# Picks' two-part rows laid out by contraction slice, picked ends compared on GpSimd, and the first four weight units split in another order

## The chip, the cores and the metric

The kernel runs on one core of one Trainium2 chip. The metric is the device time of one execution in microseconds (us), taken as the median of several runs. A profile is one further execution whose instructions are recorded; its own span and time stand beside the median below. The engines are TensorE (PE, with its weight loads as PEld), VectorE (DVE), ScalarE (ACT), GpSimd (POOL) and the queue engine SyncE (SP).

## The reference, cut to what matters

A graph network layer on 256 nodes with 8192 edges is followed by a feed-forward layer with 256 routed experts. Only the first 1024 edges have edge weights of their own kind: 128 "hh", 640 "oo", 256 "ho".

```python
x = x + gnn(layernorm(x)); x = x + ffn(layernorm(x))
# gnn, n_f = layernorm(x), 256 x 1024
feat = concatenate([n_f[edge_src], n_f[edge_dst]], axis=1)          # per edge, 2048 wide
e_hh = relu(feat[:128] @ W_hh + b_hh)                               # W_hh is 2048 x 1024
e_oo = relu(feat[128:768] @ W_oo + b_oo)
e_ho = relu(feat[768:] @ W_ho + b_ho)                               # here: all the rest
logit = (e_f @ W_a + b_a)[:, 0]; alpha = softmax of logit over edges with the same dst
z_f = segment_sum(alpha * n_f[edge_src], edge_dst)
new = relu(concatenate([n_f, z_f]) @ W_hn + b_hn)  (first 64 nodes),  W_on, b_on (the others)
# ffn: top-4 experts of 256 by hashed keys, each silu(x @ down) @ up
```

The change touches the first tile of 128 edges, which alone uses W_hh, and what stands beside it.

## The kernel before, in words

Every float32 product is made of two parts: a value is split into a high part (rounded to the type fp32r) and a low part (value minus high part), and three products (high x high, low x high, high x low) are summed in PSUM.

**Weights** come in 20 units of 4096 columns on 128 partitions. Unit u goes to slot s = u % 2 as its n-th use, n = u // 2. SP loads it in two halves into `raw`; ACT makes each half's high part (`hi(s, n)`, line 583, into `whi`), DVE the low part (`lo(s, n)`, line 795, into `wlo`), and TensorE may then use it. SP's wait before loading the next use of a slot half is for DVE's `lo` of the half before (lines 436 and 437). Units 0 to 3, which are `(0,0)`, `(1,0)`, `(0,1)`, `(1,1)` as slot and use, hold W_hh; the two W_hh halves for source and destination are uses 0 and 1.

**The first tile's features.** DVE makes the layer norm `nf` (line 826). TensorE turns `nf` by 8 transposes per tile of 128 nodes (`turn(0, t)`, line 1257), for all later edges. For the first 128 edges, a one-hot matrix `head_pick` (in the buffer `ohx`) of the 128 source and 128 destination numbers is made by four compares (`pick`, line 842, DVE), and `nf` split in `nf_hi` (ACT, line 589) and `nf_lo` (DVE, line 850), both in slot 1 of `wlo`. 32 matmuls of 256 columns (line 1278) give the features, already turned: for each of 8 contraction slices c, two node tiles t and two parts. The stationary operand is a slice with a step of 8 numbers (32 bytes) through a row of `nf_hi` or `nf_lo`. After slices 0 to 3 and again after 4 to 7 ACT takes the high part of the features to `tab_dst` (line 593) and DVE the low part (line 856).

**The first tile's edges.** TensorE multiplies the features with units 0 and 1 (48 matmuls of 512 columns, lines 1287 to 1289), turns the edge numbers, multiplies with units 2 and 3 (48 more), adds the bias, and then starts `project(1, 0)` with unit 4. DVE then runs `dot(0)` (line 988), sorts the other edges into buckets (`in_windows`, up to line 882), and TensorE counts them (line 1333) after two slices of `project(1, 0)` and ranks them (lines 1340 to 1346) after four; ACT and DVE go on from the ranks (lines 623, 900 to 918).

**Order.** Each engine's order is written out by hand; there is no scheduler. `turn_hi`/`turn_lo` (lines 574, 833) are the two parts of the turned `nf`. GpSimd starts with two long broadcasts of edge numbers by its own DMA queue (line 475, 320 KB each, into `idx_b`), makes the constants, and later compares (line 518) and runs its own long loops (lines 532 to 544).

## Time and profile before

| what | value |
|---|---|
| median of 3 runs | 761.04 us (759.07 to 761.8) |
| time of the profiled execution | 758.95 us |
| its span | 757.2 us |
| PE busy | 710.9 us, 94% of the span |
| DVE, ACT, POOL busy | 510.9, 367.0, 215.3 us |
| shares of the chain that ended last (page, part 4) | PE 64%, POOL 14%, DVE 8%, ACT 6% |
| bytes read from HBM | 112.74 MB |

A time in the rows below is in us from the start of the span. The profiled execution is 2.1 us under the median of the runs, and 1.75 us lie between its span and its time. Line numbers are those of the kernel printed above.

### The profile page before, as it was taken

How to read it: one execution, taken by the hardware profiler on the slowest of the kernel's cores; microseconds unless marked ns; L12 is line 12 of the kernel's file. 1: busy time of each engine (PE TensorE's matmuls, PEld its weight loads, DVE VectorE, ACT ScalarE, POOL GpSimd, SP SyncE). 2: the span in 40 equal slices, each digit the busy share in tenths (PEclk: the TensorE clock that was granted, in tenths of full speed). 3: DMA queues.
4: the chain of work that ended last, by engine and by line, in shares of the span. 5: the costliest groups of instructions: out<-in, count | busy, mean ns of one | idle time of the engine just before them, and what ended most of it. 6: DMA issues, size and time to landing. Idle time of an engine off the chain costs nothing.

```text
span 757.2 us, 9554 instructions
## 1 busy us (share of the span) xinstructions
PE 710.9 (94%) x3325; PEld 560.4 (74%) x3325; DVE 510.9 (67%) x706; ACT 367.0 (48%) x435; POOL 215.3 (28%) x329
## 2 busy tenths in 40 slices
PE   3999999997979989899799999999999999999998
PEld 3877776785555656587677888888888888888886
DVE  6897797597999999638878464544564544565543
ACT  3754989647646653017435244343344343344340
POOL 3373668798898804800000000000000000000000
PEclk9999999999989999699979999999999999999999
DMA  8785233341000006406905645456645356645411
GB/s 317 277 319 216 112 111 113 112 177 46 1 1 1 0 1 235 167 0 239 316 14 178 238 142 191 148 201 222 212 137 192 144 201 222 220 137 188 157 73 57
DMA packets 50058, 114.21 MB, mean 151 GB/s; under 512 B 2245, under 2 KB 35397, under 8 KB 44906
## 3 DMA queue, kind: packets, MB, share of 16 engines
q1 hardware_dynamic: 49418, 112.95, 41.5%
q0 software_dynamic: 160, 0.66, 0.2%
q8 instruction: 18, 0.29, 0.2%
q10 hardware_dynamic: 448, 0.20, 0.1%
q14 instruction: 14, 0.11, 0.0%
HBM read 112.74 MB, written 1.05 MB: 150 GB/s over the span
## 4 chain that ended last, share of the span: by engine, by line
PE 64%; POOL 14%; DVE 8%; issue 6%; ACT 6%; DMA 2%; DVEq 0%; SPq 0%; ACTq 0%
PE ps L1287 18%; PE ps L1289 17%; PE ps L1288 17%; POOL peak L539 5%; POOL oh_src L541 4%; POOL pen L544 4%; PE ps L1257 3%; DVE wlo L795 3%; ACT chunk_col L641 2%; PE ps L1587 1%; ACT chunk_gap L636 1%; PE ps L1523 1%; ACT whi L583 1%; DMA raw<-n_L_ffn_values_down_dram 1%; PE ps L1278 1%
## 5 line engine op out<-in xcount | busy, mean ns | idle before, releaser
L795 DVE TENSOR_TENSOR wlo<-raw,whi 128x2048 fp32r<-128x2048 f32 x104 | 235.3, 2288 | 67.1 <-ACT whi L583 66.3
L583 ACT ACTIVATE whi<-raw 128x2048 fp32r<-128x2048 f32 x104 | 195.9, 1911 | 90.7 <-PE ps L1289 65.9
L1287 PE MATMUL ps<-whi,nT 128*128 128x512 f32 x392 | 156.2, 399 | 1.4 <-ACT act_g L758 1.4
L1289 PE MATMUL ps<-wlo,nT 128*128 128x512 f32 x392 | 152.9, 390 | 0.0
L1288 PE MATMUL ps<-whi,nT 128*128 128x512 f32 x392 | 152.8, 390 | 0.0
L988 DVE SCALAR_TENSOR_TENSOR ps<-ps,xt 128x1024 f32<-128x1024 f32 x80 | 97.5, 1219 | 5.9 <-PE ps L1313 5.0
L1287 PE MATMUL ps<-whi,gT_hi 128*128 128x512 f32 x240 | 93.6, 390 | 0.0
L1289 PE MATMUL ps<-wlo,gT_hi 128*128 128x512 f32 x240 | 93.4, 389 | 0.0
L1288 PE MATMUL ps<-whi,gT_lo 128*128 128x512 f32 x240 | 93.4, 389 | 0.0
L1221 DVE TENSOR_TENSOR gw<-act_g,route 128x512 f32<-128x512 f32 x32 | 20.7, 688 | 106.8 <-ACT act_g L758 106.8
L1287 PEld LDWEIGHTS ps<-whi,nT 128*128 128x128 f32 x392 | 73.6, 188 | 18.3 <-issue 2.3
L1289 PEld LDWEIGHTS ps<-wlo,nT 128*128 128x128 f32 x392 | 73.6, 188 | 15.8
L1288 PEld LDWEIGHTS ps<-whi,nT 128*128 128x128 f32 x392 | 73.7, 188 | 14.3
L758 ACT ACTIVATE act_g<-ps 128x1024 f32<-128x1024 f32 x16 | 16.4, 1028 | 126.3 <-PE ps L1289 126.3
L1311 PE MATMUL ps<-tab_src,ring 128*128 x148 | 66.7, 450 | 11.2 <-DVE ps L988 5.2
L532 POOL TENSOR_SCALAR chunk_col<-iota,keep 128x74 f16<-128x74 f16 x58 | 52.5, 926 | 32.3 <-DVE keep L918 16.5
L1313 PE MATMUL ps<-tab_dst,ring 128*128 x148 | 60.1, 406 | 0.0
L1287 PEld LDWEIGHTS ps<-whi,gT_hi 128*128 128x128 f32 x240 | 45.0, 188 | 9.6 <-issue 0.4
L1289 PEld LDWEIGHTS ps<-wlo,gT_hi 128*128 128x128 f32 x240 | 45.0, 188 | 9.4
L1288 PEld LDWEIGHTS ps<-whi,gT_lo 128*128 128x128 f32 x240 | 45.0, 188 | 9.3
L1311 PEld LDWEIGHTS ps<-tab_src,ring 128*128 128x128 f32 x148 | 29.1, 197 | 30.6 <-issue 26.0
L539 POOL TENSOR_SCALAR peak<-iota,slot_idx 128x64 f16<-128x64 f16 x74 | 39.4, 532 | 11.1 <-DVE slot_idx L957 4.5
(268 smaller groups left out, 928.1 us busy)
## 6 DMA issues: line engine op xcount, KB each, us to landing
raw<-n_L_ffn_values_down_dram SPq DMA_DIRECT2D x16, 2048.0 KB, 8.3
raw<-in_L_ffn_values_up_dram SPq DMA_DIRECT2D x16, 2048.0 KB, 7.5
raw<-in_L_gnn_W_hh_dram SPq DMA_DIRECT2D x8, 1024.0 KB, 8.9
raw<-in_L_gnn_W_oo_dram SPq DMA_DIRECT2D x8, 1024.0 KB, 6.0
raw<-in_L_gnn_W_ho_dram SPq DMA_DIRECT2D x8, 1024.0 KB, 4.7
raw<-in_L_gnn_W_hn_dram SPq DMA_DIRECT2D x8, 1024.0 KB, 4.8
raw<-in_L_gnn_W_on_dram SPq DMA_DIRECT2D x8, 1024.0 KB, 5.1
xt<-in_x_dram SPq DMA_DIRECT2D x4, 512.0 KB, 7.3
```

Source lines behind the costliest of these rows:

```text
L532: last = nc.gpsimd.tensor_scalar(chunk_col[:, n % 2, j % CHUNK, 0:WN], iota16[:, 0:WN], keep[:, 2, j:j + 1], keep[:, 0, j:j + 1], ALU.is_e ...
L539: nc.gpsimd.tensor_scalar(same[:, w % 2, :], iota16[:, 1:NH + 1], slot_idx[:, 1, w:w + 1], None, ALU.is_equal).then_inc(win_same, 1)
L541: nc.gpsimd.tensor_scalar(oh_src[:, w, :], iota16[:, 1:NH + 1], slot_idx[:, 0, w:w + 1], None, ALU.is_equal).then_inc(win_src, 1)
L544: nc.gpsimd.tensor_scalar(pen[:, w, :], same[:, w % 2, :], 1.0, -NEVER, ALU.subtract, ALU.mult).then_inc(win_pen, 1)
L583: nc.scalar.activation(half(whi, s, j, down), half(raw, s, j, down), ACT.Copy)\
L795: nc.vector.tensor_tensor(half(wlo, s, j, down), half(raw, s, j, down), half(whi, s, j, down).bitcast(F32), ALU.subtract)\
L988: nc.vector.scalar_tensor_tensor(out=bank(q, 2), in0=bank(q, 2), scalar=0.0, in1=wa_b[:], op0=ALU.max, op1=ALU.mult, accum_out=logit[:, i: ...
L1287: nc.tensor.matmul(o, a_hi, b_hi, start=start, stop=False)
L1288: nc.tensor.matmul(o, a_lo, b_hi, start=False, stop=False)
L1289: return nc.tensor.matmul(o, a_hi, b_lo, start=False, stop=stop)
L1311: nc.tensor.matmul(bank(q + h), hot[:, 0, :], src_rows[:, bass.ds(a + h * HALF, HALF)], start=True, stop=False)
L1313: last = nc.tensor.matmul(bank(q + h), hot[:, 1, :], dst_rows[:, bass.ds(b + h * HALF, HALF)], start=False, stop=True)
```

## The change

Four things are changed; line numbers of the new file differ by 9 to 15.

1. `nf_hi` and `nf_lo` are written in the order (slice c, row q): ACT and DVE read `nf` with a step of 8 numbers, and the stationary operand of the 32 picking matmuls is contiguous.
2. The four compares of `pick` go from DVE to GpSimd, at the end of its constants, and GpSimd's two long broadcasts are issued behind them.
3. TensorE does `turn(0, 1)` behind the picking matmuls instead of ahead of them.
4. ACT and DVE take the features' first half between the two halves of unit 0, and split unit 2 (ACT) and units 2 and 3 (DVE) before the parts of the turned `nf` and the bias.

```diff
-        nf_hi, nf_lo = (wlo[:, 1, NT * D * k:NT * D * (k + 1)].rearrange("p (t n) -> p t n", t=NT) for k in range(2))
+        nf_hi, nf_lo = (wlo[:, 1, NT * D * k:NT * D * (k + 1)].rearrange("p (t c q) -> p t c q", t=NT, c=C)
+                        for k in range(2))
+        nf_by_c = nf[:].rearrange("p t (q c) -> p t c q", c=C)
 # GpSimd
-            for a, ends in enumerate((src, dst)):
-                pool.dma_start(idx_b[:, a, P:HEAD * P], ends[P:HEAD * P].partition_broadcast(P))\
-                    .then_inc(batch_loaded, 16)
 ...  the constants
+            pool.wait_ge(first_batch, 32)
+            for a in range(2):
+                for j, number in enumerate((row_no[:, 0:1], node[:, 1:2])):
+                    last = nc.gpsimd.tensor_scalar(head_pick[:, j * N + a * P:j * N + (a + 1) * P], idx_b[:, a, 0:P],
+                                                   number, None, ALU.is_equal)
+            last.then_inc(picker_ready, 1)
+            for a, ends in enumerate((src, dst)):
+                pool.dma_start(idx_b[:, a, P:HEAD * P], ends[P:HEAD * P].partition_broadcast(P))\
+                    .then_inc(batch_loaded, 16)
 # ACT
-                nc.scalar.activation(nf_hi[:, t, :], nf[:, t, :], ACT.Copy).then_inc(nfhi_ready, 1)
-            hi(0, 0, first=True)
-            for h in range(2):
+                nc.scalar.activation(nf_hi[:, t, :, :], nf_by_c[:, t, :, :], ACT.Copy).then_inc(nfhi_ready, 1)
+            hi(0, 0, first=True, parts=(0,))
+            feature_hi(0)
+            hi(0, 0, first=True, parts=(1,))
+            feature_hi(1)
             hi(1, 0, first=True)
+            hi(0, 1)
             for t in range(NT):
                 turn_hi(0, t)
             act.wait_ge(small_loaded, 16 * 6)
             nc.scalar.activation(bias_hi[:], bias[:], ACT.Copy).then_inc(bias_ready, 1)
-            hi(0, 1)
             hi(1, 1)
 # DVE
-            pick()
-                nc.vector.tensor_tensor(nf_lo[:, t, :], nf[:, t, :], nf_hi[:, t, :].bitcast(F32), ALU.subtract)\
+                nc.vector.tensor_tensor(nf_lo[:, t, :, :], nf_by_c[:, t, :, :], nf_hi[:, t, :, :].bitcast(F32), ALU.subtract)\
-            lo(0, 0)
-            for h in range(2):
+            lo(0, 0, parts=(0,))
+            feature_lo(0)
+            lo(0, 0, parts=(1,))
+            feature_lo(1)
             lo(1, 0)
-            for t in range(NT):
-                turn_lo(0, t)
 ...
             lo(0, 1)
+            lo(1, 1)
+            for t in range(NT):
+                turn_lo(0, t)
             (bias_lo)
-            lo(1, 1)
 # TensorE
-            for t in range(NT):
-                turn(0, t)
+            turn(0, 0)
 ...
-                                                parts[part][:, t, :].rearrange("p (q c) -> p c q", c=C)[:, c, :],
+                                                parts[part][:, t, c, :],
 ...
+            turn(0, 1)
```

On TensorE, from its first transpose to the first matmul with W_hh. Before:

```order
L1257 MATMUL ps<-ident,nf 128x128 [waits norm_ready,consts]
L1257 MATMUL ps<-ident,nf 128x128 x7
L1257 MATMUL ps<-ident,nf 128x128 [waits norm_ready]
L1257 MATMUL ps<-ident,nf 128x128 x7
L1278 MATMUL ps<-ohx,wlo 128x256 [waits nflo_ready,picker_ready]
L1278 MATMUL ps<-ohx,wlo 128x256
L1278 MATMUL ps<-ohx,wlo 128x256 [waits nflo_ready]
L1278 MATMUL ps<-ohx,wlo 128x256 x29
L1287 MATMUL ps<-whi,tab_dst 128x512 [waits lo_ready0,featlo_ready,consts]
```

After:

```order
L1267 MATMUL ps<-ident,nf 128x128 [waits norm_ready,consts]
L1267 MATMUL ps<-ident,nf 128x128 x7
L1287 MATMUL ps<-ohx,wlo 128x256 [waits nflo_ready,picker_ready]
L1287 MATMUL ps<-ohx,wlo 128x256
L1287 MATMUL ps<-ohx,wlo 128x256 [waits nflo_ready]
L1287 MATMUL ps<-ohx,wlo 128x256 x29
L1267 MATMUL ps<-ident,nf 128x128 [waits norm_ready]
L1267 MATMUL ps<-ident,nf 128x128 x7
L1297 MATMUL ps<-whi,tab_dst 128x512 [waits lo_ready0,featlo_ready,consts]
```

The second group of eight transposes has moved behind the 32 picking matmuls.

On DVE, from the picks to the copy of the edge numbers ahead of unit 4 (`idx_col`). Before:

```order
L842 TENSOR_SCALAR ohx<-idx_b,small 128x128 [waits first_batch,consts]
L842 TENSOR_SCALAR ohx<-idx_b,small 128x128 x3
L850 TENSOR_TENSOR wlo<-nf,wlo 128x1024 [waits nfhi_ready] x2
L795 TENSOR_TENSOR wlo<-raw,whi 128x2048 [waits hi_ready0] x2
L856 TENSOR_TENSOR tab_dst<-ps,tab_dst 128x1024 [waits feathi_ready] x2
L795 TENSOR_TENSOR wlo<-raw,whi 128x2048 [waits hi_ready1] x2
L833 TENSOR_TENSOR nT<-ps,nT 128x8x128 [waits turned_hi] x2
L966 CAST idx_rowf<-idx_rows 64x256 [waits idx_loaded,consts]
L795 TENSOR_TENSOR wlo<-raw,whi 128x2048 [waits hi_ready0] x2
L969 TENSOR_TENSOR bias_lo<-bias,bias_hi 5x1024 [waits bias_ready]
L795 TENSOR_TENSOR wlo<-raw,whi 128x2048 [waits hi_ready1] x2
L972 COPY idx_col<-ps 128x128 [waits smallT]
```

After:

```order
L854 TENSOR_TENSOR wlo<-nf,wlo 128x1024 [waits nfhi_ready] x2
L810 TENSOR_TENSOR wlo<-raw,whi 128x2048 [waits hi_ready0]
L861 TENSOR_TENSOR tab_dst<-ps,tab_dst 128x1024 [waits feathi_ready]
L810 TENSOR_TENSOR wlo<-raw,whi 128x2048 [waits hi_ready0]
L861 TENSOR_TENSOR tab_dst<-ps,tab_dst 128x1024 [waits feathi_ready]
L810 TENSOR_TENSOR wlo<-raw,whi 128x2048 [waits hi_ready1] x2
L974 CAST idx_rowf<-idx_rows 64x256 [waits idx_loaded,consts]
L810 TENSOR_TENSOR wlo<-raw,whi 128x2048 [waits hi_ready0] x2
L810 TENSOR_TENSOR wlo<-raw,whi 128x2048 [waits hi_ready1] x2
L848 TENSOR_TENSOR nT<-ps,nT 128x8x128 [waits turned_hi] x2
L980 TENSOR_TENSOR bias_lo<-bias,bias_hi 5x1024 [waits bias_ready]
L982 COPY idx_col<-ps 128x128 [waits smallT]
```

The picks are gone, the features' first half stands between the halves of unit 0, and the turned `nf` and the bias stand behind unit 3. ACT's order moves in the same way, with the turned `nf` and the bias between units 2 and 3.

## Rows read from the trace of the kernel before

**Rows 1.** The chain that ended last: start, duration, what, with its count.

```profile
1.26 6.81 DMA xt<-in_x_dram
...
15.39 7.90 PE ps L1278 x32
...
53.42 0.56 PE ps L1333 x16
...
79.27 1.24 DVE tab_src L982
...
390.54 1.84 PE ps L1699 x16
```

**Rows 2.** Timeline of the start: start, duration, engine, line, operation, count, [idle before].

```profile
11.15 1.53 DVE L826 TENSOR_SCALAR nf<-xt,mv,ln 128x1024 f32<-128x1024 f32 x2
12.00 2.00 ACT L589 ACTIVATE wlo<-nf 128x1024 fp32r<-128x1024 f32 x2 [1.87 <-DVE nf L826]
...
12.60 0.87 DVE L842 TENSOR_SCALAR ohx<-idx_b,small 128x128 fp32r<-128x128 int32 x4
...
13.38 2.35 DVE L850 TENSOR_TENSOR wlo<-nf,wlo 128x1024 fp32r<-128x1024 f32 x2
...
23.32 1.03 ACT L593 ACTIVATE tab_dst<-ps 128x1024 fp32r<-128x1024 f32 x1 [2.81 <-PE ps L1278]
...
24.24 3.71 ACT L583 ACTIVATE whi<-raw 128x2048 fp32r<-128x2048 f32 x2
24.38 1.23 DVE L856 TENSOR_TENSOR tab_dst<-ps,tab_dst 128x1024 fp32r<-128x1024 f32 x1 [2.62 <-ACT tab_dst L593]
...
26.18 4.50 DVE L795 TENSOR_TENSOR wlo<-raw,whi 128x2048 fp32r<-128x2048 f32 x2 [0.57 <-ACT whi L583]
...
35.38 0.50 PE L1287 MATMUL ps<-whi,tab_dst 128*128 128x512 f32 x1 [0.78 <-DVE wlo L795]
```

**Rows 3.** Waits of DVE in the first 48 us: us in total, times, longest.

```profile
DVE tab_dst L856 <- ACT tab_dst L593: 2.8, 2, 2.6
...
DVE wlo L795 <- ACT whi L583: 0.8, 2, 0.6
```

**Rows 4.** By line and window: ns min/median/max, first and last start.

```profile
L1278 PEld LDWEIGHTS ps<-ohx,wlo x32: 312/337/341, 15.1 to 22.7; 128*128 128x128 f32 x32
...
L1257 PE MATMUL ps<-ident,nf x11: 273/417/417, 13.2 to 15.1; 128*128 128x128 f32 x11
...
L1257 PE MATMUL ps<-ident,nf x8: 421/421/478, 378.1 to 379.7; 128*128 128x128 f32 x8
...
L1257 PE MATMUL ps<-ident,nf x8: 270/274/276, 387.6 to 388.4; 128*128 128x128 f32 x8
...
L518 POOL TENSOR_SCALAR ohx<-idx_b,small x8: 602/1258/10582, 33.0 to 51.2; 128x128 fp32r<-128x128 int32 x8
```

**Rows 5.** DVE groups by shape: count | busy us, mean ns | idle before.

```profile
L914 DVE TENSOR_REDUCE slot<-place 128x58 f32<-128x928 f32 x1 | 1.9, 1862 | 0.0
...
L1111 DVE TENSOR_REDUCE peak<-oh_dst 128x74 f32<-128x592 f32 x1 | 0.8, 769 | 0.0
```

**Rows 6.** DMA: us to landing; GpSimd's queue in 6.5 to 8.1 (packets, MB, share).

```profile
idx_b<-in_dst_dram ACTq DMA_DIRECT2D x1, 64.0 KB, 7.1
...
q0 software_dynamic: 31, 0.16, 23.8%
...
raw<-in_L_gnn_W_hh_dram SPq DMA_DIRECT2D x1, 1024.0 KB, 4.7
...
raw<-in_L_gnn_W_oo_dram SPq DMA_DIRECT2D x1, 1024.0 KB, 6.1
```

**Rows 7.** Timeline of DVE behind the first tile's edges.

```profile
47.90 1.23 DVE L988 SCALAR_TENSOR_TENSOR ps<-ps,xt 128x1024 f32<-128x1024 f32 x1
...
51.13 1.12 DVE L882 TENSOR_TENSOR in_bucket<-bucket,iota 128x928 f16<-128x928 f32 x1
...
57.57 1.12 DVE L893 TENSOR_TENSOR earlier<-count,below 58x928 f16<-58x928 f16 x1
```

More of the change, by code:

```diff
@@ L588, in _, with feature_hi @@
                 act.wait_ge(norm_ready, t + 1)
-                nc.scalar.activation(nf_hi[:, t, :], nf[:, t, :], ACT.Copy).then_inc(nfhi_ready, 1)
-            hi(0, 0, first=True)
-            for h in range(2):
+                nc.scalar.activation(nf_hi[:, t, :, :], nf_by_c[:, t, :, :], ACT.Copy).then_inc(nfhi_ready, 1)
+            def feature_hi(h):
                 act.wait_ge(feat_done, h + 1)
@@ L834, in turn_lo, with feature_lo @@
                                         ALU.subtract).then_inc(turned_lo, 1)
-            def pick():
-                dve.wait_ge(consts, 6)
-                dve.wait_ge(first_batch, 32)
-                for a in range(2):
-                    for j, number in enumerate((row_no[:, 0:1], node[:, 1:2])):
-                        last = nc.vector.tensor_scalar(head_pick[:, j * N + a * P:j * N + (a + 1) * P], idx_b[:, a, 0:P],
-                                                       number, None, ALU.is_equal)
-                last.then_inc(picker_ready, 1)
             layer_norm(1, range(NT))
-            pick()
             for t in range(NT):
                 dve.wait_ge(nfhi_ready, t + 1)
-                nc.vector.tensor_tensor(nf_lo[:, t, :], nf[:, t, :], nf_hi[:, t, :].bitcast(F32), ALU.subtract)\
+                nc.vector.tensor_tensor(nf_lo[:, t, :, :], nf_by_c[:, t, :, :], nf_hi[:, t, :, :].bitcast(F32), ALU.subtract)\
                     .then_inc(nflo_ready, 1)
-            lo(0, 0)
-            for h in range(2):
+            def feature_lo(h):
                 dve.wait_ge(feathi_ready, h + 1)
```

## The prediction

> **What bounds the kernel now.** I read the chain that ended last first. Of its shares on the page (in the table above) TensorE holds 64% and GpSimd 14%, nearly all of it behind the stage that is changed. In its pieces by time [rows 1], in the first 24 us the chain runs over the second half of x (landed at 8.07), the layer norm and the picking matmuls: 7.90 us for 32, or 247 ns each, of only 256 columns. The reader should see that this is far from TensorE's price for 256 columns: 1.84 us for 16 later ones, 115 ns each [rows 1]. The by-line view tells why: the weight load of a picking matmul takes 337 ns, and its stationary operand is read with a step of 32 bytes [rows 4].
>
> Then comes the timeline of the start [rows 2] and DVE's waits [rows 3]. In the first 48 us DVE waits only for ACT in its own chain behind the layer norm, 2.8 + 0.8 = 3.6 us; all else from the second `nf_lo` (ends 15.73) to `dot(0)` (47.90) [rows 2, 7] is work, 32.2 - 3.6 = 28.6 us. TensorE waits 0.78 us, for DVE, ahead of unit 2 [rows 2]. So both must be followed: a stage given to TensorE is worth something only if DVE's `dot(0)` also comes earlier.
>
> The place where both meet is the bucket count. DVE has `in_bucket` ready at 51.13 + 1.12 = 52.25, TensorE begins to count at 53.4, a slack of 1.1 us; the ranking waits for 57.57 + 1.12 = 58.69 and TensorE comes at 59.6, slack 0.9 [rows 1, 7]. What follows hangs on the ranks: ACT, DVE's sort, then the four `tab_src` parts, the last ending at 80.5 [rows 1], for which TensorE waits. So **the shift of the ranking is the shift of the end**, unless the later GpSimd loop changes it.
>
> **The change part by part.**
>
> *The long broadcasts.* GpSimd's queue moved 0.16 MB between 6.5 and 8.1 us, 24% of the DMA engines' time [rows 6]; x's second half landed at 8.07. Without it x lands earlier: 24% of 1.6 us, 0.4 us. Bounds are 0 and 1.3 (8.09 less 6.80, where DVE has done the first half of x). I take 0.4. The broadcasts are now issued near 11 us and first needed beyond 40 us (ACT's unit 3, GpSimd's `head_destinations`); a queue time of 11 us would still cover that. Behind them on GpSimd stands only `both_ready`.
>
> *The compares.* DVE loses 0.87 us [rows 2], but `nf_lo` waits for ACT's `nf_hi`, so 0.3 us at most is won. GpSimd's unobstructed price is 0.60 us [rows 4]: from the landing at 1.27 + 7.1 = 8.4 [rows 6] four take until 10.8. They are needed at 15. Cost nothing, covered by `nf_lo`. If the cover goes, see the third rival.
>
> *The strided reads* go from TensorE to ACT and DVE. No row shows either engine reading single words 32 bytes apart. The nearest is a reduction over a step of 232 bytes: 1.862 us for 928 numbers, 2.0 ns each, against 0.769 for 592 in order, 1.3 each [rows 5], so 0.7 ns more for each. Bounds for `nf_lo`: 1.22 (today) and 2.6 (today's doubled, and a little); I take 1.22 + 1024 x 0.7 ns = 1.9. For `nf_hi`: 1.05 to 2.1; with no row of ACT I take a third of the way, 1.4. The Trainium skill speaks against the change here: "SBUF — State Buffer" (its remark on cachelines) says that each access that crosses to a new 16-byte line pays, and "Vector Engine (DVE) Microarchitecture Reference", 5.2, gives 1.73 ns per column with one source hopping every element. By that `nf_lo` would take 1.85 us and the sum would stand; a reader who trusted the old 1.22 would forecast 1.8 us less for it.
>
> With x 0.4 earlier ACT starts at 11.6: `nf_hi` ends at 13.0 and 14.4, `nf_lo` at 14.95 and **16.8** (before 15.73).
>
> *The picking matmuls.* Two run at 15, the other 30 from 16.85. What is their price? Before, TensorE worked without a pause from 12.1, and its transposes fell from 417 to 273 ns shortly before 15 us [rows 4]. 421 ns is the same transpose at granted clock 0.50 and 274 at 1.00, at 378 and 388 us; so it rose from 1.2 to 2.4 GHz there, and all picking ran at 2.4. After, TensorE has eight transposes, then almost nothing until 16.85. I take it that it is at 1.2 GHz until about 20: 256 columns in 0.213 us. Bounds: 0.115 at once, and 0.215 to the end. Then feature half 0 is done at 16.85 + 14 x 0.213 + 0.15 = 20.0 (before 19.4), half 1 at 21.9, and the eight transposes at 22.7. So contiguous rows gain 0.7 on the whole, not 4.2.
>
> *The features between the halves.* ACT takes half 0 by 21.05 (1.03 each); DVE, done with unit 0's first half at 19.05, idles 2.05 us; its part ends at 22.35. TensorE starts W_hh at 22.8 (23.1 before). ACT splits the second half of unit 0 by 22.95, so DVE idles 0.65 more. Unit 0 ends on DVE at 25.3, feature half 1 at 26.5, unit 1 at 30.95 (before 26.18 + 4.50 = 30.7).
>
> *The other order.* DVE is done with unit 2 at 35.7. The second half of unit 2 is issued only when unit 0 is done, at 25.3 (before about 20.4), and lands after 4.7 to 6.1 us [rows 6]; I take 5.0. ACT then does it by 32.2, the turned `nf` (two of 1.0, as half a feature takes) and the bias by 35.1, unit 3's first half by 37.0: DVE idles 1.3 us. Idle in all: 2.05 + 0.65 + 1.3 = 4.0, and `dot(0)` comes at 16.8 + 28.6 + 4.0 = 49.4, allowing 0.2 for the hand-overs 49.6, **1.7 later**. TensorE loses its 0.78 wait and starts `project(1, 0)` at 47.5 (47.7 before); it then waits for DVE's buckets, 49.6 + 4.35 = 54.0, beyond its 53.2. What is late next is DVE, and 1.1 and 0.9 us of its delay fall into the slack named above: 1.7 - 0.9 = **+0.8 at the ranking**, +0.1 for the restart of TensorE behind the wait. GpSimd's eight compares, 19.9 us before, begin near 43 instead of 33 and end near 63, ahead of the sort's 69.
>
> **The sum** against the profiled execution: 758.95 + 0.9 = 759.85. That execution lies 2.1 us below the median of the runs, so I forecast 761.9.
>
> **The rivals.**
>
> *1. The strided reads cost nothing.* For it: ACT and DVE have no strided row at 32 bytes; against it the reduction's row and TensorE's own 337 ns. `nf_lo` ends at 15.1, all moves 1.7 earlier, features at half clock still: `dot(0)` 47.6, ranking 1.0 before today's. If TensorE is at 2.4 GHz too, half 0 is done 1.3 us sooner, and with x 1 us earlier the ranking is 3 us before. Time 760.0, to 758.0 at the best.
>
> *2. Strided reads at twice the price, loads at 6.1 us.* `nf_hi` 2.1, `nf_lo` 2.6: it ends near 20, half 0 at 22.3, `dot(0)` at 52 to 53: +3 to +4.2. It decides from the point where `nf_lo` ends beyond 16, since DVE has no other slack before `dot(0)` than 0.9. 764.0 to 765.3.
>
> *3. The compares come late (slower).* GpSimd's compares range from 602 to 10582 ns, the longest while DVE ran its `lo` back to back [rows 4]: DVE shuts it out. They start at 8.4 and must be through before `nf_lo` starts at 13; the margin is 2.2 us, with DVE's `nf` (11.15 to 12.7) in it [rows 2]. If one compare is left then, it lies until DVE's first pause, near 19.5, and the picking begins there: 2.7 us later than in my sum, features 3.3 later, time 765.2. "SBUF — State Buffer", on who interferes with whom, in the Trainium skill, states such a lock for two SBUF inputs; the 10.58 us agree.
>
> *4. It doesn't do what it says:* TensorE's pace at 1.2 GHz makes contiguous loads worthless, nothing else changes: picking 32 x 0.215, half 0 as in the sum, half 1 at 23.4. DVE decides anyway; 762.2, inside the forecast.
>
> **How the numbers follow.** Forecast with its neighbour 4: 0.55, 760.5 to 763.2. Rival 1: 0.22. Rival 2: 0.10. Rival 3: 0.06. Something that I see no row for, half to each side: 0.07. GpSimd's loop from 142 to 264, whose locked-out compares fall differently, and the runs' own spread of 2.7 us add about a microsecond either way. The range 758.5 to 764.6 leaves out rival 3, most of 2 and the best of 1. 0.5% is 3.8 us, about what can be told from no change: faster (below 757.2) 0.11, slower (above 764.8) 0.11, same 0.78.
>
> **What would show it.** Right: `nf_hi` near 1.4 and `nf_lo` near 1.9; picking matmuls at two paces, 0.21 then about 0.12; DVE idle for ACT in three places, one ahead of unit 3; a TensorE wait for `in_bucket`; `dot(0)` near 49.6. Wrong: a changed duration nowhere but in the weight loads (rival 1), a compare of several us (rival 3), or an end that moves by another amount than the ranking. The forecast fails most easily at the two prices taken between far bounds, ACT's strided read and the clock.

## The result and the profile after

| | before | after |
|---|---|---|
| median of 20 runs each, on one chip | 760.12 us (758.06 to 762.33) | 763.04 us (760.62 to 767.68) |
| ratio, with its 95% interval | | 1.0041 (1.0028 to 1.0053) |
| time and span of the profiled execution | 758.95, 757.2 us | 760.62, 758.9 us |
| PE busy | 710.9 us | 707.1 us |

The change makes the kernel slower by 0.4%, 2.9 us between the medians: within the 0.5% called "same", but its interval lies wholly above 1. The forecast was +0.9 us, 761.9 us with a range of 758.5 to 764.6. Range and sign held; the size is three times what the sum gave. That the time itself is only 1.1 us above the forecast is in part luck: the forecast started from a median before of 761.04 us, and the 20 runs of the comparison gave 760.12.

The chain that ended last of the kernel after (start, duration, what) answers to [rows 1]:

```profile
1.25 7.42 DMA xt<-in_x_dram
...
12.68 2.14 ACT wlo L598
14.84 4.00 DVE wlo L854 x2
18.89 3.33 PE ps L1287 x14
...
30.64 2.29 DVE wlo L810
32.95 6.43 DMA raw<-in_L_gnn_W_hh_dram
39.40 1.93 ACT whi L592
```

Before, TensorE's 32 picks stood in this chain with 7.90 us. Now ACT's and DVE's parts of `nf` stand there, then only the first 14 picks behind them, and later a weight load, `raw`, directly ahead of ACT's and DVE's split of it. x itself landed 0.6 us later than before (7.42 us where 6.81 stood).

The timeline of the kernel after, for the same pieces as [rows 2] and [rows 7] (start, duration, engine, line, names, [idle before]):

```profile
11.84 1.54 DVE L841 TENSOR_SCALAR nf<-xt,mv,ln 128x1024 f32<-128x1024 f32 x2
12.68 4.08 ACT L598 ACTIVATE wlo<-nf 128x1024 fp32r<-128x1024 f32 x2 [1.87 <-DVE nf L841]
14.84 3.99 DVE L854 TENSOR_TENSOR wlo<-nf,wlo 128x1024 fp32r<-128x1024 f32 x2 [1.47 <-ACT wlo L598]
...
23.30 1.22 DVE L861 TENSOR_TENSOR tab_dst<-ps,tab_dst 128x1024 fp32r<-128x1024 f32 x1 [2.26 <-ACT tab_dst L603]
25.09 2.29 DVE L810 TENSOR_TENSOR wlo<-raw,whi 128x2048 fp32r<-128x2048 f32 x1 [0.57 <-ACT whi L592]
38.67 2.29 DVE L810 TENSOR_TENSOR wlo<-raw,whi 128x2048 fp32r<-128x2048 f32 x1 [1.15 <-ACT whi L592]
41.36 2.29 DVE L810 TENSOR_TENSOR wlo<-raw,whi 128x2048 fp32r<-128x2048 f32 x1 [0.39 <-ACT whi L592]
51.57 1.21 DVE L998 SCALAR_TENSOR_TENSOR ps<-ps,xt 128x1024 f32<-128x1024 f32 x1
54.67 1.12 DVE L890 TENSOR_TENSOR in_bucket<-bucket,iota 128x928 f16<-128x928 f32 x1
61.18 1.12 DVE L901 TENSOR_TENSOR earlier<-count,below 58x928 f16<-58x928 f16 x1
```

Read it against the old rows in order. `nf` is 0.69 us later (11.15 before). Each `nf_hi` takes 2.04 us where 1.0 stood, each `nf_lo` 2.0 where 1.2 stood, so the second `nf_lo` ends at 18.8 instead of 15.73: 3.1 us late. `dot(0)` is 3.67 us later, `earlier`, which the ranking needs, 3.61.

TensorE's weight loads of the picking matmuls show why contiguous rows gave it little at first. The line view of the kernel after (ns min/median/max, first and last start), from 12 to 22 us and from 22 to 24 us:

```profile
L1287 PEld LDWEIGHTS ps<-ohx,wlo x17: 285/330/338, 17.0 to 21.8; 128*128 128x128 f32 x17
...
L1287 PEld LDWEIGHTS ps<-ohx,wlo x16: 188/192/287, 21.8 to 23.7; 128*128 128x128 f32 x16
```

The contiguous load takes 330 ns until about 22 us, hardly less than the 337 ns of the strided one in [rows 4], and 192 ns after that. The profile prints a granted clock of 1.00 for the whole stretch, so the clock is read from durations here. By the pair of transposes in [rows 4], 421 and 274 ns at granted clock 0.50 and 1.00, TensorE is at 1.2 GHz first and at 2.4 GHz from about 22 us: its eight transposes ahead of the picks take 421 ns, those behind them 276. It did those first eight, sat idle for 2.25 us, did two picks and sat idle for 1.13 more. The 330 ns need not be the price of the load alone: the weight loads of the transposes are recorded with 0.22 to 0.23 us in the same slow stretch, and no run separates a load from the matmul that it overlaps.

The ranking gives each edge its place in its bucket; DVE's first operation with these ranks is `total_i`. It starts 2.78 us later than before, and what follows on DVE up to the GpSimd loop between 2.7 and 2.8. The profiled execution gave 1.1 us of this back behind 180 us; its granted clock from 290 to 400 us was 0.91 where the one before had 0.89. The medians, 2.9 us apart, don't show such a gift.

### The profile page after: what moved, and what is told of

It reads as the page before. It is cut to its first block, busy times and chain, and to the rows that moved or that the text cites. A ratio compares the mean times of both kernels' runs of the same rounds, so it can differ in the third digit from the quotient of the medians.

```text
span 758.9 us, 9553 instructions
## 1 busy us (share of the span) xinstructions
PE 707.1 (93%) x3325; PEld 556.5 (73%) x3325; DVE 511.9 (67%) x702; ACT 369.0 (49%) x435; POOL 212.6 (28%) x333
## 3 DMA queue, kind: packets, MB, share of 16 engines
HBM read 112.74 MB, written 1.05 MB: 150 GB/s over the span
## 4 chain that ended last, share of the span: by engine, by line
PE 59%; POOL 14%; DVE 10%; ACT 6%; issue 6%; DMA 4%; DVEq 0%; SPq 0%; ACTq 0%
PE ps L1297 17%; PE ps L1299 16%; PE ps L1298 16%; POOL peak L548 5%; POOL pen L553 5%; POOL oh_src L550 4%; DVE wlo L810 4%; PE ps L1267 2%; ACT whi L592 2%; ACT chunk_col L656 2%; ACT chunk_gap L651 1%; PE ps L1597 1%; DMA raw<-n_L_ffn_values_down_dram 1%; PE ps L1632 1%; DMA xt<-in_x_dram 1%
## 5 line engine op out<-in xcount | busy, mean ns | idle before, releaser
L1299 PEld LDWEIGHTS ps<-wlo,nT 128*128 128x128 f32 x392 | 73.6, 188 | 15.8
L541 POOL TENSOR_SCALAR chunk_col<-iota,keep 128x74 f16<-128x74 f16 x58 | 52.5, 922 | 26.5 <-PE ps L1366 15.8
```

The costliest lines, as they stand in the source:

```text
L541: last = nc.gpsimd.tensor_scalar(chunk_col[:, n % 2, j % CHUNK, 0:WN], iota16[:, 0:WN], keep[:, 2, j:j + 1], keep[:, 0, j:j + 1], ALU.is_e ...
L1299: return nc.tensor.matmul(o, a_hi, b_lo, start=False, stop=stop)
```

## The experiments

Twelve experiments ran, in three groups of four; two of them repeat a kernel. The column "ranks, shift" gives the start of `total_i` against 62.11 us in the kernel before; it and the two columns to its left are read from one profile each.

| kernel | second `nf_lo` ends | `dot(0)` | ranks, shift | ratio to before (95%) |
|---|---|---|---|---|
| before | 15.7 | 47.90 | 0 | 1 |
| after | 18.8 | 51.57 | +2.78 | 1.0041 (1.0028 to 1.0053) |
| after_again | 19.0 | 52.96 | +4.17 | 1.0033 (1.0019 to 1.0046) |
| after_old_rows | 16.2 | 49.63 | +0.84 | 1.0015 (1.0000 to 1.0029) |
| before_rows_only | 18.1 | 49.22 | +1.32 | 1.0002 (0.9982 to 1.0021) |
| after_old_order | 18.8 | 49.50 | +1.61 | 1.0023 (1.0011 to 1.0035) |
| before_order_only | 15.8 | 49.29 | +0.51 | 1.0008 (0.9994 to 1.0023) |
| after_early_broadcast | 18.1 | 50.89 | +2.11 | 1.0018 (1.0006 to 1.0030) |
| before_picks_only | 16.1 | 48.67 | +0.77 | 1.0003 (0.9989 to 1.0017) |
| before_unit2_first | 15.6 | 47.84 | -0.05 | 0.9997 (0.9984 to 1.0011) |
| high_parts_first | 15.7 | 46.51 | -1.38 | 0.9987 (0.9970 to 1.0004) |
| high_first_again | 15.7 | 46.50 | -1.39 | 0.9964 (0.9952 to 0.9977) |
| high_first_by_slice | 18.5 | 48.34 | +0.44 | 1.0001 (0.9986 to 1.0015) |
| high_first_bias_pool | 15.7 | 47.27 | -1.38 | 0.9986 (0.9973 to 0.9999) |

A ratio has an interval of about 1 us either way. The shift of the ranks comes from one profile: in the two of high_parts_first it agrees to 0.01 us, in the two of the kernel after it differs by 1.4 us, for a reason found below (the landing of one load). Shift and ratio agree within the ratio's interval but for after_again, whose profile is slower than its ratio, and high_first_again, whose ratio is better than its shift.

### Part by part: the rows and the order

My theory after the result (A) was that the strided reads on ACT and DVE are the loss, and only because the new order leaves nothing to cover them; the rival (B) was that the order alone is. I undid each in the kernel after and did each alone in the kernel before.

**after_old_rows**, part 1 undone:

```diff
-nc.scalar.activation(nf_hi[:, t, :, :], nf_by_c[:, t, :, :], ACT.Copy)
+nc.scalar.activation(nf_hi[:, t, :], nf[:, t, :], ACT.Copy)
 ...  nf_lo and the stationary operand in the same way
```

> The kernel after, with part 1 undone: nf_hi and nf_lo written in nf's own order, the picking matmuls' weight loads with a step of 32 bytes. The whole computation stays. Theory A (the price of the strided reads on ACT and DVE, 2.09 and 2.02 us where 1.0 and 1.2 stood, is the loss, because in the new order nothing covers it): the second nf_lo ends near 16.4 instead of 18.8, the features' first low part starts near 21 instead of 23.3, dot(0) near 49 to 50 instead of 51.6, the ranking 0 to 1.3 us behind that of the kernel before; median 0 to 1.3 us above before (ratio 1.000 to 1.002). Theory B (the new order of units alone is the loss, DVE waits for ACT in it whatever the rows cost): dot(0) stays within 0.7 us of 51.6, median 2.5 to 3 us above before (1.0035 to 1.004). Open beside it: the pace of strided picking matmuls at a granted clock of half speed, 0.24 us apart if the loads are hidden there, 0.35 or more if not.

`nf_lo` ends at 16.2 and the ranks come 1.94 us earlier than in the kernel after. Theory A's numbers hold (49.63, +0.84), and theory B, which had `dot(0)` within 0.7 us of 51.6, is wrong. The open question has an answer too, in the chain and line views:

```profile
L1285 PEld LDWEIGHTS ps<-ohx,wlo x32: 312/338/341, 15.2 to 23.2; 128*128 128x128 f32 x32
```

```profile
16.23 7.53 PE L1285 MATMUL ps<-ohx,wlo 128*128 128x256 f32 x30 [0.22 <-DVE wlo L852]
```

Thirty strided picks take 7.53 us, 0.25 each. Of the contiguous ones in the kernel after the first 14 took 3.33 us, 0.24 each, and the other 16 the 1.9 us that were left of 5.23, 0.12 each. So in the slow stretch contiguous rows are worth next to nothing to TensorE, and behind it half of a pick. How long the slow stretch lasts is not the layout's doing: 30 contiguous picks took 5.23 us in the kernel after, but 6.51 in after_early_broadcast below, where they began 0.7 us earlier and loads of 330 ns lasted until about 24 us.

**before_rows_only**, part 1 alone:

```diff
-nc.scalar.activation(nf_hi[:, t, :], nf[:, t, :], ACT.Copy)
+nc.scalar.activation(nf_hi[:, t, :, :], nf_by_c[:, t, :, :], ACT.Copy)
 ...  nf_lo and the stationary operand in the same way
```

> The kernel before with part 1 alone (rows by contraction slice). The whole computation stays. Theory A in its full form (the price matters only together with the new order): nf_lo ends near 18.2 instead of 15.7, 2.5 us later, but DVE's 2.6 us wait ahead of the features' first low part shrinks to near 0, since it splits all of unit 0 meanwhile; unit 1 ends on DVE near 31.0 (30.7 before), dot(0) near 48.2 to 48.5, the ranking at most 0.1 us later; median within 0.5 us of before (ratio 0.9995 to 1.0007). A rival, A2 (the price comes through in any order): dot(0) at 50 or later, median 1.5 to 2.5 us above before (1.002 to 1.0033). Theory B: no change, as A.

The expectation misreads a row: DVE's wait of 2.6 us in the kernel before stands ahead of the second low part of the features, at 24.38 in [rows 2], and ahead of the first there is one of only 0.2:

```profile
20.54 1.23 DVE L856 TENSOR_TENSOR tab_dst<-ps,tab_dst 128x1024 fp32r<-128x1024 f32 x1 [0.21 <-ACT tab_dst L593]
```

In before_rows_only the long one shrank to 1.80 us, and not to nothing, since the second half of the features came 1.3 us later:

```profile
18.21 6.38 PE L1280 MATMUL ps<-ohx,wlo 128*128 128x256 f32 x30 [1.12 <-DVE wlo L852]
```

```profile
22.66 1.23 DVE L858 TENSOR_TENSOR tab_dst<-ps,tab_dst 128x1024 fp32r<-128x1024 f32 x1
24.62 1.03 ACT L595 ACTIVATE tab_dst<-ps 128x1024 fp32r<-128x1024 f32 x1 [2.00 <-PE ps L1280]
25.68 1.22 DVE L858 TENSOR_TENSOR tab_dst<-ps,tab_dst 128x1024 fp32r<-128x1024 f32 x1 [1.80 <-ACT tab_dst L595]
```

The picks began 2.8 us later than in [rows 1] and saved only 1.5 of it; the ranks are 1.32 us late, `dot(0)` 49.22. So A's "only together with the order" is wrong, and A2's "50 or later" as well. The ratio, 1.0002, can't show 1.3 us but doesn't exclude it either (its upper end is 1.6 us).

**after_old_order**, part 4 undone, and **before_order_only**, part 4 alone (the diff shows the undoing):

```diff
-            hi(0, 0, first=True, parts=(0,))
-            feature_hi(0)
-            hi(0, 0, first=True, parts=(1,))
-            feature_hi(1)
+            hi(0, 0, first=True)
+            (both halves of the features)
 ...  the turned nf and the bias back ahead of unit 2, on DVE in the same way
```

> The kernel after with part 4 undone on ACT and DVE (both halves of unit 0 ahead of the features, the turned nf and the bias where they stood), and parts 1 to 3 kept. The whole computation stays. Theory A: nf_lo still ends near 18.8, but DVE's unit 0 covers the wait for the features: unit 1 ends near 31.5 (30.7 before, 32.9 after), dot(0) near 48.8, the ranking 0 to 0.2 us later than before; median 0 to 0.5 us above before. Rival A2 (the price comes through in any order): dot(0) near 50.5 or later, median 2 us or more above before. Theory B: median as before.

> The kernel before with part 4 alone on ACT and DVE. The whole computation stays. nf_lo ends at 15.7 as before. Theory A (order and price together): DVE has an idle stretch of about 2.5 us behind the first half of unit 0 as it has one of 2.6 now, unit 1 ends near 30.9, and no wait of over 0.5 us ahead of unit 3; dot(0) near 48.2, median within 0.5 us of before. Theory B (the order alone is the loss): DVE waits for ACT in three places, dot(0) at 50 or later, median 2 to 3 us above before.

Undone, the ranks come 1.17 us earlier; alone, 0.51 us later. Neither theory's numbers hold. Undone, A had `dot(0)` near 48.8 and the ranks at most 0.2 us late, A2 had 50.5 or later, and B a median as before; measured were 49.50, +1.61 and a ratio of 1.0023. Alone, A had 48.2 and B 50 or later, and 49.29 was measured. A had put the order alone at nothing and B the rows alone; both have a price of their own. The timeline of before_order_only shows the order's:

```profile
36.21 2.29 DVE L800 TENSOR_TENSOR wlo<-raw,whi 128x2048 fp32r<-128x2048 f32 x1 [0.87 <-ACT whi L583]
39.08 2.29 DVE L800 TENSOR_TENSOR wlo<-raw,whi 128x2048 fp32r<-128x2048 f32 x1 [0.57 <-ACT whi L583]
```

DVE waits for ACT ahead of both halves of unit 3, and `dot(0)` is 1.39 us late; 0.9 of it goes into the slack ahead of the ranking.

### The landing of x

In five profiles with the long broadcasts behind GpSimd's constants, x's second half reached DVE at 8.65 to 8.84 us; in those with the broadcasts in front, at 7.89 to 8.21 (nine profiles by the end). I had forecast the opposite.

**after_early_broadcast**:

```diff
 # GpSimd, ahead of the constants
+            for a, ends in enumerate((src, dst)):
+                pool.dma_start(idx_b[:, a, P:HEAD * P], ...).then_inc(batch_loaded, 16)
 ...  the constants, the four compares
-            for a, ends in enumerate((src, dst)):
-                pool.dma_start(idx_b[:, a, P:HEAD * P], ...).then_inc(batch_loaded, 16)
```

> The kernel after with GpSimd's two long broadcasts in front again, its four compares still behind the constants; the whole computation stays. In the three kernels with the late broadcasts DVE began on x's second half at 8.65 to 8.72, in the three with early ones at 8.04 to 8.10. Theory X (the early broadcasts do not delay x, their absence does): x's second half at 8.05 to 8.1, nf 0.6 us earlier than after, compares still through by 12.5, dot(0) near 51.0, the ranking 2.2 us behind that of before instead of 2.8, median 1.5 to 2.6 us above before. Rival X2 (what shifts x is GpSimd's own compares or its constants, not the queue): x at 8.65 or later, median as after, about 2.9 us above. Rival X3 (my first forecast: a broadcast ahead costs x 0.4 us): x at 9.0.

**before_picks_only**, part 2 alone:

```diff
-            layer_norm(1, range(NT))
-            pick()
+            layer_norm(1, range(NT))
 ...  the compares on GpSimd behind its constants, the broadcasts behind them
```

> The kernel before with part 2 alone (the four compares on GpSimd at the end of its constants, the long broadcasts behind them); the whole computation stays. Theory X: x at 8.65 to 8.7, nf 0.6 us later, nf_lo without the 0.3 us of the picks: ends near 16.0; features, unit 1 and the ranking 0.3 to 0.6 us later; median 0.3 to 0.6 us above before (ratio 1.0004 to 1.0008). Rival (the compares block or are blocked for longer): a compare of over 1 us, or nf_lo at 17 or later.

The chain's row on x, in after_early_broadcast and then in before_picks_only:

```profile
1.26 6.61 DMA xt<-in_x_dram
```

```profile
1.26 7.42 DMA xt<-in_x_dram
```

Moving nothing but the two broadcasts to the front brings x 0.8 us earlier and the ranks from +2.78 to +2.11; in the kernel before, compares and late broadcasts together cost 0.77 (0.3 to 0.6 expected), with x's row at 7.42 again. Theory X holds, X2 and X3 fall, and so does my first term (0.4 us the other way). In the window from 5.5 to 8.0 us the kernels before and after compare so (us, busy time and count of PE, PEld, DVE, ACT and POOL, granted clock, DMA share, GB/s):

```profile
5.50:8.00 2.50, 0.00 (x0) 0.00 (x0) 1.29 (x2) 0.00 (x0) 1.82 (x11) 1.00 0.73 241
```

```profile
5.50:8.00 2.50, 0.00 (x0) 0.00 (x0) 1.29 (x2) 0.00 (x0) 1.50 (x9) 1.00 0.68 195
```

There is 0.11 MB less traffic in all, but the early broadcasts themselves moved 0.14 MB in that window. What SP's own queue had moved when x's second half landed says more (packets, MB, share), in the kernel before up to 8.07 us and in the kernel after up to 8.67:

```profile
q1 hardware_dynamic: 305, 1.19, 46.8%
```

```profile
q1 hardware_dynamic: 341, 1.48, 51.7%
```

x is 1.05 MB of each (two loads of 512 KB). So before it landed, 0.14 MB of what SP had queued behind it, mostly weights, had been moved in the kernel before, and 0.43 MB in the kernel after. after_early_broadcast, the kernel after with the broadcasts in front, stood at 1.16 MB when x landed at 7.87 us. At 8.07 us, where x was complete in the kernel before, SP's queue had moved no less in the kernel after, 1.27 MB. So with the broadcasts behind, x does lose its share, to what SP itself has queued behind it. Why the early broadcasts hold that back, no run here tells; that stays open.

### Who sets the ranking, and a better version

**before_unit2_first** took one piece of part 4:

```diff
-            for t in range(NT):
-                turn_hi(0, t)
-            (bias_hi)
             hi(0, 1)
+            for t in range(NT):
+                turn_hi(0, t)
+            (bias_hi)
             hi(1, 1)
 ...  on DVE in the same way
```

> The kernel before with one piece of part 4: ACT and DVE split unit 2 ahead of the two parts of the turned nf and the bias, but leave these ahead of unit 3. The whole computation stays. In the kernel with all of part 4 DVE waited 0.87 us ahead of unit 3, because ACT still had the turned nf and the bias to do. Theory C (TensorE sets the ranking in the kernel before, DVE has 0.9 us in hand, and it is unit 3 ahead of the turned nf that costs DVE its wait): TensorE's 0.78 us wait ahead of unit 2 is gone, DVE has no new wait over 0.3 us ahead of unit 3, project(1, 0) and the ranking 0.6 to 0.8 us earlier; median 0.5 to 0.9 us below before (0.9988 to 0.9993). Rival (any such move only trades one wait for another): DVE waits 0.8 us or more ahead of unit 3 all the same, median within 0.3 us of before or above it.

Theory C fell, and the wait of DVE that its rival named did not come either. TensorE's wait of 0.78 us ahead of unit 2 went, and one of 0.62 us for unit 3 took its place (chain, then timeline, of before_unit2_first):

```profile
35.20 2.27 DVE nT L833 x2
37.46 1.12 DVE bias_lo L969
38.59 2.21 DVE wlo L795
```

```profile
40.84 0.50 PE L1287 MATMUL ps<-whi,tab_dst 128*128 128x512 f32 x1 [0.62 <-DVE wlo L795]
```

DVE does the same work in another order and TensorE meets it one unit later. I conclude that the start gets shorter only if DVE's own chain does.

**high_parts_first** tries that. Its picks don't wait for `nf_lo`: each half takes the high parts of both tiles first. Four more things differ from the kernel before, all named in the last lines of the diff.

```diff
-            for c in range(C):
-                for t in range(NT):
-                    (wait for nf_lo of tile t) for part in range(2): matmul
+            for h in range(2):
+                for part, there in enumerate((nfhi_ready, nflo_ready)):
+                    for t in range(NT):
+                        (wait for there) for c in range(4 * h, 4 * h + 4): matmul
 ...  rows as before; compares on GpSimd, broadcasts in front; turn(0, 1) behind;
 ...  features between the halves of unit 0; unit 2 ahead of the turned nf
```

> A version meant to beat both, built on the kernel before. The whole computation stays. The rows keep nf's order (cheap reads on ACT and DVE); the compares are on GpSimd, broadcasts in front; TensorE takes in each half of the features first the high parts of both node tiles, then the low ones, so that its strided weight loads begin with nf_hi (13.0) and not with nf_lo; the second eight transposes behind; features between the halves of unit 0; unit 2 ahead of the turned nf, unit 3 behind it. Theory: what the start needs is picking that does not wait for nf_lo; picking from 13.8 at 0.25 us each, half 0 done at 17.8 (19.3 before), half 1 at 21.8 (23.3), DVE idle under 1.5 us ahead of the features, dot(0) near 46, TensorE the bound: W_hh from 22.8 without a wait, ranking 1.0 to 1.3 us earlier than before; median 758.6 to 758.9 beside 759.9. Rival (the restart at half speed and the compares on GpSimd give it back): half 0 at 19 or later, median as before.

```profile
13.92 7.97 PE L1283 MATMUL ps<-ohx,wlo 128*128 128x256 f32 x32
```

```profile
19.13 1.23 DVE L857 TENSOR_TENSOR tab_dst<-ps,tab_dst 128x1024 fp32r<-128x1024 f32 x1 [0.79 <-ACT tab_dst L600]
```

The picks take the same 8 us but start at 13.92 instead of 15.1 [rows 4]. DVE's waits for ACT behind the layer norm come to 0.40 + 0.39 + 0.79 + 0.58 + 0.42 = 2.6 us, where [rows 3] had 3.6, and its compares are gone. The ranks come 1.38 us earlier, 0.1 us more than the upper end of the forecast. Of this, 0.55 us is the start of TensorE on W_hh, 22.56 instead of 23.11, and 0.78 us the wait ahead of unit 2, which is gone. The picks by parts were not tried without the other four moves, so their own share isn't shown.

**high_first_again** is the same kernel once more, beside **after_again**, the kernel after (no edit in either):

> The kernel of high_parts_first once more, unchanged, to narrow its interval (it stood at 0.9987, 0.9970 to 1.0004) beside the kernel after on the same chip. The whole computation stays. Theory (the ranking comes 1.38 us earlier than before, and what lies between ranking and end adds only scatter): the ranking again 1.2 to 1.6 us earlier, ratio 0.9975 to 0.9990. Rival (the gain is scatter of the clock's falls): ratio 1.000 or above.

> The kernel after, unchanged, on the same chip as the repeated version. The whole computation stays. x's second half at 8.65 to 8.75, nf_hi 2.0 to 2.1 us each, ranking 2.6 to 2.9 us behind before; ratio 1.003 to 1.005.

The ranks come 1.39 us earlier again, and the ratio, 0.9964 (0.9952 to 0.9977), now lies wholly under 1, and beyond the 0.9975 to 0.9990 that was expected. On the same chip the kernel after stood at 1.0033. The gain's sign is settled by the second run; its size isn't: -1.0 us and -2.7 us in the two groups, where the ranks say -1.4 both times.

after_again brought something new, a shift of +4.17 in its profile (I had expected 2.6 to 2.9). Its chain:

```profile
30.82 2.30 DVE wlo L810
33.14 7.64 DMA raw<-in_L_gnn_W_hh_dram
40.80 1.93 ACT whi L592
42.75 2.29 DVE wlo L810
```

The second half of unit 3 landed after 7.64 us where it took 6.43 in the first profile, 1.2 us more, and its issue came 0.2 later; the ranks moved by 1.39. In the new order DVE's other work stands behind this split and none ahead of it, so **each microsecond by which that load is late is a microsecond at the ranks**. The load took 6.26 to 6.43 us in the four other profiles with this order, so 7.64 is the one outlier of five. That is the other thing that the order costs: it exposes a transfer's scatter. At the end it is not seen: the median of this run stood 2.4 us above that of before.

**high_first_by_slice** asks whether rows by slice pay once the picks don't wait for `nf_lo`. It also has both groups of transposes ahead and takes all high parts before the low ones:

```diff
 # high_parts_first, and
-            turn(0, 0)
+            for t in range(NT):
+                turn(0, t)
-            (picks by half)
+            for part in range(2): for t in range(NT): for c in range(C): matmul
 ...  nf_hi and nf_lo written by slice
```

> high_parts_first with the rows by contraction slice (part 1 of the change) and both groups of transposes ahead, so that TensorE works from 12.1 on; all high parts first, then the low ones. The whole computation stays. Theory D (the strided read only changes engines, and DVE is as near to the bound as TensorE): nf_lo ends near 18.2, the features are complete near 19.5 to 20 (21.8 in high_parts_first), W_hh starts near 21.7 (22.9 there), but DVE is 0.3 to 1.0 us later than there at unit 1 and TensorE waits for it ahead of unit 2 or 3; ranking 0.3 to 1.1 us earlier than before, so 0.3 to 1 us worse than high_parts_first; ratio 0.9988 to 1.0000. Rival E (contiguous rows pay once the picks do not wait for nf_lo): ranking 1.4 us or more earlier than before, ratio under 0.998.

```profile
15.66 5.19 PE L1284 MATMUL ps<-ohx,wlo 128*128 128x256 f32 x32
22.79 0.47 PE L1294 MATMUL ps<-whi,tab_dst 128*128 128x512 f32 x1 [1.94 <-DVE tab_dst L859]
```

Rival E falls for this build. TensorE saves 2.8 us of picking and then waits 1.94 us for DVE; the ranks are 0.44 us later than before and 1.82 later than with rows in order. That is worse than D's forecast, which had them 0.3 to 1.1 us earlier than before. The 1.82 us are not the rows' price alone: the picks began at 15.66 instead of 13.92, behind the second transposes, and half 0 was complete only at 20.4, since all high parts of both halves stood ahead of it. Rows by slice in the order of high_parts_first were not tried.

**high_first_bias_pool** moves one operation off DVE:

```diff
-            nc.vector.tensor_tensor(bias_lo[:], bias[:], bias_hi[:].bitcast(F32), ALU.subtract)
+            nc.gpsimd.tensor_tensor(bias_lo[:], bias[:], bias_hi[:].bitcast(F32), ALU.subtract)
```

> high_parts_first with the bias's low part on GpSimd, behind its copy of the turned nf, instead of DVE. The whole computation stays. Theory F (DVE's work is what TensorE follows from unit 2 on; GpSimd is idle there): DVE saves 1.1 us ahead of unit 3, TensorE loses its 0.46 us wait there, ranking 1.5 to 1.9 us earlier than before (1.38 in high_parts_first). Rival G (GpSimd's operation is held up while DVE runs its splits back to back, as the compare of 10.6 us in the kernel before): it ends after 45.2, TensorE waits for the bias, ranking later than in high_parts_first; if it lasts 5 us or more, as late as before or later.

```profile
36.06 6.74 POOL L532 TENSOR_TENSOR bias_lo<-bias,bias_hi 5x1024 fp32r<-5x1024 f32 x1
```

```profile
L809 DVE TENSOR_TENSOR wlo<-raw,whi x4: 2275/2367/4324, 36.0 to 44.9; 128x2048 fp32r<-128x2048 f32 x4
```

GpSimd's operation of 1024 columns took 6.74 us among DVE's splits, and one of these took 4.32 us instead of 2.28. It ended at 42.79 (spans on GpSimd are rough, but its next operation starts there), so TensorE did not wait for the bias (G's threshold wasn't reached), but DVE gave back what it had saved: `dot(0)` came at 47.27 where 46.51 stood, and the ranks stand at -1.38 with it and without it. F, with 1.5 to 1.9 us, falls too. The Trainium skill, "SBUF — State Buffer", on who interferes with whom, says that of a VectorE operation with two SBUF inputs and a GpSimd operation that reads SBUF the later one is blocked until the other is through. The rows agree: the split began at 40.65, GpSimd's operation ended at 42.79, and a split of 2.28 us from there would end at 45.07; it ended at 44.97.

## Why the prediction was right in sign and short in size

**x, forecast -0.4 us, measured +0.69.** The step that failed is the argument "without the broadcasts x lands earlier: 24% of 1.6 us", with bounds of 0 and -1.3. It was a bound on one side only, and the value lay beyond it. after_early_broadcast shows the sign in the same kernel. Of the 2.0 us by which `dot(0)` missed the forecast (51.57 for 49.6), this is 1.1.

**The strided reads, forecast 1.4 and 1.9 us each, measured 2.09 and 2.02 us.** The line view of the kernel after:

```profile
L598 ACT ACTIVATE wlo<-nf x2: 2047/2088/2129, 12.7 to 14.7; 128x1024 fp32r<-128x1024 f32 x2
```

```profile
L854 DVE TENSOR_TENSOR wlo<-nf,wlo x2: 2003/2024/2045, 14.8 to 16.8; 128x1024 fp32r<-128x1024 f32 x2
```

DVE's term was nearly right. ACT's was the weak one: with no row of ACT I took a third of the way between the bounds, and the price was the upper bound. The estimate of 1.85 us for DVE, worked out in the prediction from the 1.73 ns per column of the Trainium skill ("Vector Engine (DVE) Microarchitecture Reference", 5.2), was near as well; the measured 2.02 us decides. The miss up to the end of `nf_lo` is 18.83 - 16.8 = 2.0 us: 1.1 from x, 0.9 from these two.

**From there to `dot(0)`, forecast 49.6 - 16.8 = 32.8 us, measured 51.57 - 18.83 = 32.7.** This part of the sum held as a whole, and most of its steps did. Half 0 of the features was done 3.4 us behind `nf_lo` (3.2 forecast), the first picks at half speed, the rest at full. DVE's waits for ACT, behind `nf_lo`:

```profile
DVE tab_dst L861 <- ACT tab_dst L603: 2.3, 1, 2.3
DVE wlo L810 <- ACT whi L592: 2.1, 3, 1.2
```

4.4 us in four places, 4.0 forecast in three; the one ahead of unit 3's first half is 1.15 (1.3 forecast). The fourth, 0.39 us ahead of unit 3's second half, comes from a term that was too small: I took 5.0 us for a load of half a unit, and this one took 6.43, outside the 4.7 to 6.1 of [rows 6]. It cost 0.4 us here, and a still longer one 1.4 more in after_again. The sign that I had named, TensorE waiting for the buckets, is there, and beside it is a wait that the sum didn't have, 0.49 us ahead of unit 4:

```profile
49.59 0.47 PE L1297 MATMUL ps<-whi,nT 128*128 128x512 f32 x1 [0.49 <-DVE wlo L810]
...
55.85 0.63 PE L1343 MATMUL ps<-ones,in_bucket 128*58 128x1 f16 x16 [0.56 <-DVE in_bucket L890]
```

One remark of the prediction follows from none of its times, that contiguous rows gain TensorE 0.7 us on the whole. By its own times 30 picks take 21.9 - 16.85 = 5.05 us; 30 strided ones take 7.5, so the gain is 2.4, and 2.3 was measured (7.53 to 5.23). The sum didn't use the remark.

**The slack of 0.9 us ahead of the ranking.** `dot(0)` +3.67 gave ranks +2.78; in after_again +5.06 gave +4.17, in after_old_rows +1.73 gave +0.84, in before_order_only +1.39 gave +0.51, in after_early_broadcast +2.99 gave +2.11. It is 0.9 in all five, as the prediction had it. In the kernels with unit 3 behind the turned `nf` there is no such slack, since there the chain runs over TensorE at that point: +1.32 gave +1.32, +0.77 gave +0.77, +1.60 gave +1.61. In high_first_bias_pool, where DVE was held up, -0.63 gave -1.38.

**"The shift of the ranking is the shift of the end"** holds in the medians of the kernel after (+2.78, 2.9 us) and as far as ratios can tell in most others. In single profiles it doesn't: 1.1 us were returned behind 180 us in one, 1.7 us lost in another (high_first_again's profile ends 0.3 us above the span before, with ranks 1.39 us earlier).

**The compares** took 0.60 us each, from 9.02 to 11.37, four without a hold-up; rival 3 did not happen. Behind the broadcasts, in after_early_broadcast, they took 3.34 us together, and still cost nothing.

**The rivals.** Rival 2 (strided reads at twice the price) is nearest in the shift of the ranks: its ACT price was right, its DVE price (2.6) was not, and its time, 764.0 to 765.3, is 1 to 2 us beyond the median. Rival 1 (reads for nothing) is wrong; rival 4 (contiguous loads worthless at the low clock) is right for the first 16 picks only. I gave ACT's upper bound a chance of 0.10, together with slow loads, which was too little for a price that no row contradicted. That the range held is no proof of the prices in it: they missed to the slow side together, and the range was wide enough.

**By part**, each alone against the kernel before, at the ranks: rows +1.32, compares and broadcasts +0.77, order +0.51, in sum +2.60; together +2.78. That they nearly add up hides that they depend on each other. Undone in the kernel after, the rows give back 1.94 us and the order 1.17, each 0.6 to 0.7 more than its price alone. None of the three gains anything here. Moving `turn(0, 1)` was not tried alone, and neither were ACT's and DVE's strided reads apart from each other.

## What to carry to other kernels

A strided read that is moved from TensorE's weight load to the engines that feed it must be priced on both of them, and on the chain: here TensorE could take its 7.9 us of picks only behind DVE, so a gain of 2.7 us on TensorE (7.90 to 5.2) was bought with 3.1 us (0.7 of it x's) on the chain ahead of it. Start the matmuls on the operand that is ready first instead (high parts, then low ones): the kernel that did so, with four other moves, had its ranks 1.4 us earlier. Put no load directly ahead of the engine that sets the end while that engine has other work it could do first, and bound a term on both sides unless a row excludes one.

## What the runs showed of the hardware

- Two broadcasts queued by GpSimd ahead of its constants made the load of x faster, not slower: 7.89 to 8.21 us in nine profiles, 8.65 to 8.84 in the five without them. SP's queue had then moved 0.14 MB of what stood behind x, instead of 0.43 MB. The cause is open.
- ACT, copying 1024 single words 32 bytes apart, took 2.09 us where it takes 1.0 in order; DVE with one source of two read so took 2.02 where it takes 1.2. A contiguous weight load between picks of 256 columns with TensorE at 1.2 GHz was recorded with 330 ns, about as much as a strided one at 2.4 GHz (337 ns); at 2.4 GHz a contiguous one took 192 ns.
- 30 to 32 strided picks took 7.5 to 8.1 us in every kernel, with TensorE idle ahead of them or not; contiguous ones took 5.2 to 6.5 us, by how long the slow pace lasted.
- A GpSimd operation of 1024 columns took 6.74 us among DVE's splits, and one of these took 4.32 us instead of 2.28.
